# A decoder layer's jobs get times of their own, a third dense buffer, sums on POOL, and multiplications ahead of the first loads

## The reference

```python
# 1: causal linear attention, 16 heads of 64, 128 random features per head
q, k, v = heads(x @ Wq), heads(x @ Wk), heads(x @ Wv)
phi(u) = exp(u @ W_feat - sum(u * u) / 2) / sqrt(128)
y[t] = phi(q[t]) @ sum_{s<=t} outer(phi(k[s]), v[s]) / (phi(q[t]) @ sum_{s<=t} phi(k[s]) + eps)
x = layernorm(x + concat(y) @ Wo)
# 2: differential cross attention to 77 context rows, 16 heads, two softmaxes each
att = softmax(q1 k1) - lam * softmax(q2 k2)
x = layernorm(x + att @ v)
# 3: mixture of 16 experts; a token goes to 4 of them, chosen in 2 of 4 groups, plus a shared expert
weights = 2.5 * normalised sigmoid(x @ gate_w.T) of the chosen four
y = sum_e weights[e] * (silu(x @ Wg[e]) * (x @ Wu[e])) @ Wd[e]
x = layernorm(x + y + shared(x))
```

## Time and profile before

| | |
|---|---|
| median of 3 runs | 997.05 us (994.81 to 1001.26) |
| the profiled execution's own time | 1003.07 us |
| its span | 1001.3 us |
| TensorE busy | 844.2 us, 84% |
| VectorE busy | 667.8 us, 67% |
| ScalarE busy | 497.0 us, 50% |
| POOL busy | 346.1 us, 35% |
| mean granted clock of TensorE | 0.921 |

### The profile page before, as it was taken

One profiled execution on the slowest core, in us unless ns is written; L12 is line 12 of the kernel. 1 busy time (PEld: TensorE's weight loads), 2 busy tenths in 40 slices (PEclk: granted clock), 3 DMA queues, 4 the chain that ended last, 5 costly groups with the idle time before them and its releaser, 6 DMA issues.

```text
span 1001.3 us, 19630 instructions
## 1 busy us (share of the span) xinstructions
PE 844.2 (84%) x6908; PEld 627.8 (63%) x6908; DVE 667.8 (67%) x1714; ACT 497.0 (50%) x1003; POOL 346.1 (35%) x376
## 2 busy tenths in 40 slices
PE   5899978998898899899989989986497876699763
PEld 2578756866676687667768767775275664575331
DVE  4577734457777765777875576877385667664888
ACT  4777744443775443468553437720146753454221
POOL 5211100100583143139415215913314662355121
PEclk9999977999999999999999999997688998799985
DMA  8366565411121133101123221243432322323341
GB/s 297 96 166 172 136 123 139 120 49 50 38 50 52 55 97 87 41 22 31 46 75 107 80 80 32 80 175 129 153 101 91 91 88 71 98 93 113 116 153 72
DMA packets 70158, 96.65 MB, mean 97 GB/s; under 512 B 19632, under 2 KB 50480, under 8 KB 69552
## 3 DMA queue, kind: packets, MB, share of 16 engines
q1 hardware_dynamic: 63408, 78.87, 28.1%
q0 software_dynamic: 5376, 15.47, 4.2%
q10 hardware_dynamic: 1280, 1.05, 0.4%
HBM read 42.33 MB, written 33.10 MB: 75 GB/s over the span
## 4 chain that ended last, share of the span: by engine, by line
PE 49%; DVE 27%; ACT 8%; issue 6%; SPq 5%; DMA 3%; POOL 2%; ACTq 0%; DVEq 0%
PE ps L1517 23%; PE ps L1614 4%; PE ps L1617 4%; PE ps L1595 4%; SPq L692 3%; PE ps L1604 3%; DVE xmax L1378 2%; PE ps L1585 2%; PE ps L1586 2%; PE ps L1587 2%; PE ps L1574 2%; PE ps L1672 1%; DVE low_parts L1323 1%; DVE st L1188 1%; DVE yT L1497 1%
## 5 line engine op out<-in xcount | busy, mean ns | idle before, releaser
L883 POOL TENSOR_TENSOR low_parts<-square,qk 128x512 f16<-128x512 f32 x64 | 76.0, 1187 | 407.4 <-DVE qk L1325 407.3
L1323 DVE SCALAR_TENSOR_TENSOR low_parts<-ps,qk 128x512 f16<-128x512 f32 x64 | 44.1, 689 | 113.8 <-ACT square L974 109.2
L890 POOL TENSOR_TENSOR prob<-prob_full,prob 128x512 f16<-128x512 f32 x84 | 99.3, 1201 | 7.6 <-ACT prob_full L1018 6.2
L912 POOL DMA_INDIRECT rows_out<-attn_mem,dest x64 | 61.8, 966 | 111.2 <-ACT attn_mem L1069 97.5
L1517 PE MATMUL ps<-x_split,w_qkv 128*128 128x512 f16 x384 | 99.3, 397 | 0.9 <-DVE low_parts L1323 0.9
L969 ACT ACTIVATE qk<-ps 128x512 f16<-128x512 f32 x64 | 38.2, 596 | 118.9 <-PE ps L1517 113.4
L1614 PE MATMUL ps<-attn_mem 128*128 128x65 f32 x512 | 93.6, 276 | 2.7 <-issue 2.1
L1614 PEld LDWEIGHTS ps<-attn_mem 128*128 128x128 f32 x512 | 81.0, 197 | 10.8 <-issue 3.1
L1617 PE MATMUL ps<-run,attn_mem 128*128 128x65 f32 x384 | 76.5, 282 | 0.0
L985 ACT ACTIVATE attn_mem<-ps 128x512 f32<-128x512 f32 x64 | 38.5, 602 | 75.6 <-PE ps L1587 74.8
L1595 PE MATMUL ps<-attn_mem 128*128 128x128 f32 x512 | 72.4, 286 | 2.8 <-issue 2.8
(11 more groups left out here) (284 smaller groups left out, 2137.6 us busy)
## 6 DMA issues: line engine op xcount, KB each, us to landing
qk<-low_parts SPq DMA_DIRECT2D x128, 128.0 KB, 2.4
attn_mem<-rows_in SPq DMA_DIRECT2D x64, 144.0 KB, 2.4
late_mem<-ffn_w SPq DMA_DIRECT2D x17, 384.0 KB, 3.8
rows_in<-zero_row SPq DMA_DIRECT2D x32, 144.0 KB, 2.2
up_split<-late_mem SPq DMA_DIRECT2D x16, 256.0 KB, 3.3
x_stage<-xT SPq DMA_DIRECT2D x4, 512.0 KB, 4.4
down_split<-late_mem SPq DMA_DIRECT2D x16, 128.0 KB, 3.6
rows<-x SPq DMA_DIRECT2D x4, 512.0 KB, 4.6
```

The costliest lines, as they stand in the source:

```text
L883: pool.tensor_tensor(low_parts[:, n % 2, 1, :], square[:, n % 2, :], qk[:, n % 2, n // 2 % 2, 0, 1, :], ALU.subtract).then_inc(p_sql.sem, 1)
L890: pool.tensor_tensor(prob[:, n % RING, 1, :], prob_full[:, n % FULL, :], prob[:, n % RING, 0, :], ALU.subtract).then_inc(pr_low.sem, 1)
L912: pool.indirect_dma_start(rows_out[b], bass.IndirectOffsetOnAxis(ap=dest[:, i % YB, j:j + 1], axis=0), yb[:, i % YB, j, :], None).then_inc ...
L1323: dve.scalar_tensor_tensor(low_parts[:, n % 2, 0, :], bank[:, :], 1 / W_SCALE, pair[:, 0, 0, :], ALU.mult, ALU.subtract).then_inc(p_low.se ...
```

## The change

It has four parts.

1. **Jobs timed one by one.** `attention_jobs`, `merged`, `tile_jobs` and `dense_jobs` are gone. Each job gets a time of its own (start of its block or stage plus a number from the tables ATT, CHAIN or END), and the list is sorted by these times. The set of 1,190 jobs is the same.
2. **Three buffers** for the hidden rows of the dense experts in place of two; the weights `wT` move to the memory of `xv` to make room.
3. **Sums on POOL.** Two of the three adds of a `combine` move from VectorE to POOL.
4. **Ahead of the first loads** POOL fills two buffers with ones, and TensorE multiplies them: 12 products on the whole width or on half of the rows, 8 + 16 on 64 and 32 of the array's columns, 6 more on 64 columns. On VectorE a memset and a reciprocal of constants are added at setup step 12. No result uses them.

```diff
-def attention_jobs(t):
...
-    if t + 2 >= 2:
-        add("project", t + 2, H)
-    add("turn keys", t - 1, H)
-    add("q features", t, H)
-    add("state", t - 2, H)
-    add("attend", t - 1, H)
-    if t % 2 == 1:
-        add("turn output", (t - 5) // 2, PAIRS)
-    add("k features", t, H)
-    add("output", t - 3, H)
...
+ATT = dict(project=-1.94, turn_keys=1.1, q_features=0.2, values_0=0.17, values_1=0.17, state=2.57, attend=1.45,
+           turn_output=5.6, k_features=0.36, output=3.73)
+
+CHAIN = dict(out=4.28, out_d=0.239, norm1=5.03, turn=5.55, queries=5.56, scores=6.82, scores_d=0.071, maxima=9.36,
+             probs=9.86, probs_d=0.165, norm2=14.72, cross=15.45, gate=15.84, route0=15.97, up=16.24, route1=17.71,
+             route2=18.29, down=18.08, route3=19.1, prefix=19.61, dispatch=19.62, keep=19.63, ends=20.45)
...
+END = dict(out=-3.81, out_d=1.205, norm1=-0.18, turn=-0.17, queries=-0.16, scores=1.04, scores_d=0.211, maxima=8.72,
+           probs=9.4, probs_d=0.247, norm2=17.99, cross=19.47, gate=20.35, route0=20.52, up=21.03, route1=21.52,
+           route2=21.84, down=22.52, route3=21.85, weights=23.04, dense=23.67, dense_d=2.109, dense_2=1.323,
+           pick=0.65, keep=2.0, sum=4.75, sums=37.0, sums_d=1.0, sums_n=0.77)
...
+    return [job for _, _, job in sorted(jobs)] + end_jobs()
...
-        dense_h = prob_mem[:, 0:1024].rearrange("p (r t) -> p r t", r=2)
-        dense_hT = prob_mem[:, 1024:2048].bitcast(F16).rearrange("p (r a t) -> p r a t", r=2, a=2)
-        wT = prob_mem[0:WROW + NE, 2048:2304].bitcast(F16)
+        dense_h = prob_mem[:, 0:1536].rearrange("p (r t) -> p r t", r=DR)
+        dense_hT = prob_mem[:, 1536:3072].bitcast(F16).rearrange("p (r a t) -> p r a t", r=DR, a=2)
+        wT = xv[0:WROW + NE, :, :, :, :].rearrange("p g c a v -> p (g c a v)")[:, 0:TB]
...
         def _(pool):
+            pool.memset(att[:, :, :, :], 1.0).then_inc(warm.sem, 1)
+            pool.memset(low_parts[:, :, :, :], 1.0).then_inc(warm.sem, 1)
...
+                elif kind == "combine":
+                    i = NT * b + n
+                    four = yg[i % YG]
+                    pool.wait_ge(*yg_loaded[i % YG](i // YG + 1, 0))
+                    pool.tensor_tensor(four[:, 0:2, :], four[:, 0:2, :], four[:, 2:4, :], ALU.add).then_inc(paired.sem, 1)
+                    pool.wait_ge(*paired(i, 1))
+                    pool.tensor_tensor(four[:, 0, :], four[:, 0, :], four[:, 1, :], ALU.add).then_inc(paired.sem, 1)
...
                     act.wait_ge(*dn_gate(0, n + 1))
-                    if n >= 2:
-                        act.wait_ge(*dn_low(0, n - 1))
-                    act.activation(dense_h[:, n % 2, :], bank[:, :], ACT.Tanh, scale=0.5 / W_SCALE).then_inc(dn_tanh.sem, 1)
+                    if n >= DR:
+                        act.wait_ge(*dn_low(0, n - DR + 1))
+                    act.activation(dense_h[:, n % DR, :], bank[:, :], ACT.Tanh, scale=0.5 / W_SCALE).then_inc(dn_tanh.sem, 1)
...
+                if s == 12:
+                    link(dve.memset(prob_full[:, 0:2, :], 1.0))
+                    link(dve.reciprocal(prob_full[:, 2, :], prob_full[:, 1, :]))
...
-                    dve.wait_ge(*yg_loaded[i % YG](i // YG + 1, 0))
+                    dve.wait_ge(*paired(i + 1, 0))
                     four = yg[i % YG]
-                    link(dve.tensor_tensor(four[:, 0:2, :], four[:, 0:2, :], four[:, 2:4, :], ALU.add))
-                    link(dve.tensor_tensor(four[:, 0, :], four[:, 0, :], four[:, 1, :], ALU.add))
                     dve.tensor_tensor(total[:, n, :], four[:, 0, :], total[:, n, :], ALU.add).then_inc(folded.sem, 1)
...
+            pe.wait_ge(*warm(0, 2))
+            for _ in range(2):
+                for h in range(2):
+                    rows = slice(HD * h, HD * h + HD)
+                    pe.matmul(banks[3 + h][:, :], low_parts[rows, 0, 0, 0:P], low_parts[rows, 1, 0, :], start=True, stop=True)
+            for c in range(4):
+                pe.matmul(banks[0][:, P * c:P * c + P], att[:, 0, c, :], att[:, 1, c, :], start=True, stop=True)
...
+            for cols in (64, 32):
+                for c in range(4):
+                    for at in range(0, P, cols):
+                        pe.matmul(banks[2][at:at + cols, P * c:P * c + V1], att[:, 0, c, at:at + cols], att[:, 1, c, 0:V1],
+                                  start=True, stop=True)
```

More of the change, by code:

```diff
@@ L73 @@
 XG, YB, YG = 8, 3, 3
+DR = 3
 WROW = 32
 UP, DOWN = 2, 4
[L79 to L103 removed]
@@ new lines, in chain_jobs @@
+def chain_jobs(put, start, b, at):
+    for n in range(NT):
+        put(start + at["out"] + n * at["out_d"], "project out", b, n)
+    put(start + at["norm1"], "norm1", b, 0)
+    for n in range(2):
+        put(start + at["turn"], "turn stream", b, n)
+    for n in range(KD):
+        put(start + at["queries"], "queries", b, n)
+    for n in range(NT * NG):
+        put(start + at["scores"] + n * at["scores_d"], "scores", b, n)
+    put(start + at["maxima"], "turn maxima", b, 0)
+    for n in range(CHUNKS + LAG):
+        when = start + at["probs"] + n * at["probs_d"]
+        if n < CHUNKS:
+            put(when, "probs", b, n)
+        if n >= LAG:
+            for _, _, m in weighs(b, n - LAG):
+                put(when, "weigh", b, m)
+    put(start + at["norm2"], "norm2", b, 0)
+    for n in range(2):
+        put(start + at["cross"], "turn cross", b, n)
+        put(start + at["up"], "shared up", b, n)
+        put(start + at["down"], "shared down", b, n)
+    put(start + at["gate"], "gate", b, 0)
+    for n in range(4):
+        put(start + at[f"route{n}"], "route", b, n)
+    if b == DENSE:
+        put(start + at["weights"], "weights", b, 0)
+    else:
+        put(start + at["prefix"], "prefix", b, 0)
+        put(start + at["dispatch"], "dispatch", b, 0)
+        put(start + at["keep"], "keep", b, 0)
+        if b == GROUPS[GROUP_OF[b]][-1]:
+            put(start + at["ends"], "ends", GROUP_OF[b], 0)
+            put(start + at["ends"], "table", GROUP_OF[b], 0)
@@ L224, in schedule @@
     first = [(bb, c) for bb in GROUPS[0] for c in range(NT)]
-    ahead = [[] for _ in range(len(first) + 2)]
     for i, (bb, c) in enumerate(first):
-        ahead[i].append(("fetch", bb, c))
-        ahead[i + 2].append(("combine", bb, c))
+        put(END["sums"] + i * END["sums_d"], "fetch", bb, c)
+        put(END["sums"] + (i + 2) * END["sums_d"], "combine", bb, c)
         if c == NT - 1:
-            ahead[i + 2].append(("norm3", bb, 0))
-    rest = [job for part in dense[done:] for job in part]
@@ L232, in schedule @@
-    jobs += merged(rest, [job for part in ahead for job in part])
-    jobs += [("total", DENSE, c) for c in range(NT)] + [("norm3", DENSE, 0)]
-    return jobs
-def dense_jobs(e):
-    jobs = []
-    for kind, k in (("dense gate", e), ("dense up", e), ("dense weigh", e - 1), ("dense keep", e - 1),
-                    ("dense down", e - 2)):
-        if 0 <= k < NE:
-            jobs.append((kind, DENSE, k))
-    return jobs
+            put(END["sums"] + (i + 2) * END["sums_d"] + END["sums_n"], "norm3", bb, 0)
@@ L247, in job_bank @@
+    return [job for _, _, job in sorted(jobs)] + [("total", DENSE, c) for c in range(NT)] + [("norm3", DENSE, 0)]
 def job_bank(kind, b, n):
@@ L562, in decoder_layer @@
         centred = signal("centred")
+        warm = signal("warm")
         t_down = signal("t_down"); t_kept = signal("t_kept")
@@ L1814, in _ @@
                         total = banks[TOTAL_BANKS[c // 2]][:, D * (c % 2):D * (c % 2) + D]
-                        last = three_pass(total, lambda i: dense_hT[:, n % 2, i, P * c:P * c + P],
+                        last = three_pass(total, lambda i: dense_hT[:, n % DR, i, P * c:P * c + P],
                                           lambda j: (d_high, d_low)[j][:, n, :], False, n == NE - 1 and c % 2 == 1)
```

183 lines of the change are left out of this document (68 added, 115 removed).

## The result

The changed kernel takes **936.6 us** (935.20 to 937.98, four runs) against 998.28 us for the kernel before on the same chip: a ratio of 0.938, 95% interval 0.935 to 0.942. Forecast were 971 us and a range of 949 to 990. The profiled execution took 935.2 us, with a span of 933.5 us, so between the two profiles there are 67.8 us to find.

A forecast was written before the change was run, and what follows sets the result against it. It took TensorE to bound the attention blocks, large TensorE holes to mark the expert-tile stretch, VectorE to bound the tail. Terms 12 + 2 + 9 + 3 + 5 - 5 + 0 + 0 = 26 us off 997 gave 971 us, range 949 to 990.

The forecast's parts named there:

- Attention blocks, 5 us: Three attention blocks: reordered jobs close TensorE's waits for keys, a route and the gate; 5 us gain (5 loss to 15 gain).
- My clock term: From 700 to 750 us: shorter holes spare time at half clock, worth some 7 us there alone.
- rival (c): Whole kernel: the holes close, with tail 22, tiles 14, blocks 15 and no block 0 loss; 946 us, chance 0.17.
- Tail, 12 us: Summing of gathered rows: two adds per combine leave VectorE for POOL, less added VectorE waits; 12 us gain (6 to 22).
- Here the third dense buffer counts: Tail: POOL's combine waits for a fetch with a later dense keep behind it; the third buffer was named as help.
- Third buffer, 2 us: Before the first combine: the dense loop may lag one expert more, cutting TensorE's waits for POOL; 2 us gain (0 to 4).
- Last block among the tiles, 9 us (2 to 14): Last block's chain: expert tile jobs put between producers and TensorE consumers shorten waits of gate, probs and weights; 9 us gain.
- End of block 2, 3 us: Where block 2 ends: routing part 2 behind shared down, last output turn ahead of the prefix; 3 us gain (0 to 6).
- Block 0, 5 us loss: Block 0's short steps: early k features wait for moved halves in every second step; 5 us loss (0 to 10).
- Start, 0: Multiplications before the first loads: 2.5 us lost if one after another, 1.5 won if side by side; taken as 0.
- Rival (a): All pairs of steps: features starve waiting for moved halves; slower, 1028 us, middle case 1010 us, chance 0.10.
- (b): Tail and other gains: POOL and VectorE take turns on the shared port, leaving 6 and 3 us; 988 us, chance 0.15.

The follow-up runs named there:

- sums_dve2: The changed kernel with the two adds per combine back on VectorE; ratio to the kernel before 0.9511, first combine to first total 59.8 us.
- pool_only: The kernel before with only the two adds of each combine moved to POOL, two dense buffers and the old order; ratio to the kernel before 1.0139.
- two_rings: The changed kernel with two dense buffers instead of three; ratio to the kernel before 0.9384, first combine to first total 51.7 us.
- late0: The changed kernel with k features behind attend in block 0 only; ratio to the kernel before 0.9337, project out 0 at 186.9 us.
- no_warm2: The changed kernel without the multiplications before the loads and without POOL's two fills for them; ratio to the kernel before 0.9471.
- after_again: The changed kernel itself, run again on another chip as the measure there; ratio to the kernel before 0.9408.

## Why the prediction was right in direction and too small

- **Attention blocks, 5 us: the step that failed.** They gave 32.6 us. The mechanism (a wait closed by distance) is borne out by the waits that are gone; the size was taken from three single waits in the earlier trace rows. Not added up were the idle time of the whole blocks (14.2 + 12.8 + 19.3 us), of which about 15 us went, and the clock of 0.96, 0.97 and 0.95, which is some 40 us at half pace, worth 20 us at most; the busy time fell by 17 us. My clock term stood in rival (c), and there for 700 to 750 us alone. The experiments add that the moves can't be priced one by one: undoing single moves or parts costs 0.8 to 6.0 us in block 1, undoing one of the two halves 14 to 20.
- **Tail, 12 us:** 14.7. POOL's part is 10.0 us (sums_dve2). The price on VectorE was right in kind: six adds lengthened by about 0.95 us, where ten waits of 0.84 were taken, and 2.9 us of waits for POOL's second add. But the term stood as if it needed nothing else; pool_only shows a loss of 14 us without the new places. "Here the third dense buffer counts" named the wrong cover.
- **Third buffer, 2 us:** 1.9 by two_rings, but in another place: before the first combine, where the term stood, two buffers cost nothing (64.2 against 64.3 us).
- **Last block among the tiles, 9 us (2 to 14):** 15.3 from `probs` to `weights`. 12.5 us of it are idle time, near the 12.6 that stood in the sum before the discount. The gate's wait is 1.4 us, that of `weights` 4.7, where under 3 was expected. The same 845 matmuls are busy for 2.8 us less, at a clock of 1.00 instead of 0.91 up to `turn cross`.
- **End of block 2, 3 us:** nothing from project out 3 to scores (34.3 and 34.3), and ahead of it the idle time of block 3 stayed: VectorE's routing mask is no longer waited for (2.3 us before), but the last output turn waits 6.5 instead of 2.9 us. The move of this turn, which the term counted as part of a gain, cost more there.
- **Block 0, 5 us loss:** near the truth, though the two profiles show a gain of 2.9. Project out 0 starts at 182.4 to 188.3 us, mean 184.5, in the eight kernels with k features late in block 0, and at 185.4 to 192.7, mean 188.7, in the twelve with them early. The kernels differ in more than that, and late0 alone did not show it, so the 4 us stay likely and not shown.
- **Start, 0:** 0.7 us in the profile, up to 1.5 by no_warm2. The parts do run beside each other (see the end). Beside the 28 products of 65 columns the term counted ten larger ones; the change has 14 (4 of 512 columns, 4 and 6 of 128). The added memset and reciprocal on VectorE were not tried alone.
- **Rival (a)** did not come: L1584 waits 11.6 us for moved halves, and the same features waited 13.8 us before. **(b)** fell, though six of its twelve turns are there. **(c)**, 946 us at a chance of 0.17, was the right picture and still 9 us short.

## What to carry to other kernels

Before pricing waits one by one, take the idle time and the granted clock of each whole stage: here the clock alone was 24.5 of 67.8 us. Single moves of a schedule may look worthless or small (0.8 and 4.3 us in block 1, where the whole order gave 16.8), because the places depend on each other; try them together. How much of the clock a single hole takes did not come out as a rule here: a hole of 3.0 us was passed at full clock in one run, and one of 1.41 us was not in another. Moving work to an idle engine is worth nothing by itself if that engine's queue also holds a link of the loop that the work belongs to; place the two apart first.

## What the runs showed of the hardware

**Indirect DMAs beside TensorE.** In three of the five batches every kernel that issued a block's 16 indirect DMAs on POOL in one piece, 1.27 us apart, had TensorE stand for 0.3 to 2.4 us between single matmuls that wait for nothing: TensorE's timeline in after_again, then its waits in block 2.

```profile
361.17 0.38 PE L1496 MATMUL ps<-w_o,yT 128*128 128x256 f16 x2 [0.81 <-issue]
362.60 0.27 PE L1496 MATMUL ps<-w_o,yT 128*128 128x256 f16 x1 [1.05 <-issue]
```

```profile
PE ps L1496 <- issue: 7.7, 10, 1.5
```

The three dispatches cost some 40 us in all (39.7 from project out 1 to scores). On the other chips the same instructions ran without a gap. Issued in groups of eight, five and three they cost nothing on either sort. The distance inside a group is the same 1.27 us, so it is not this spacing alone that counts: in all 28 dispatches in one piece on these chips TensorE's first such stand came 7.8 to 11.1 us after the first transfer, beside the seventh to ninth of them, and the last one 20.9 to 22.6 us after it. The groups of eight, whose starts lie within 10.1 us, had none. Why is open.

**Column parts of the array.** In the changed kernel's start 48 matmul records of 65 columns in parts of 64 or 32 took 2.16 us, 0.045 us each (the profile has two records for each fp32 multiplication of the program). The eight over the whole array just ahead took 1.81 us, but they ran at a slow pace: eight of the same size took 1.00 us in block 0 of before, 0.125 each. So the parts are still nearly three times as fast, and the timeline starts them in pairs (64 columns) and fours (32) some 0.007 us apart: they run beside each other. The Trainium skill (TensorEngine Tiling (Array Packing), Key Properties) says that tiles load and multiply in parallel; the trace agrees.

```profile
6.82 1.81 PE L1508 MATMUL ps<-attn_mem 128*128 128x65 f32 x8
8.55 2.16 PE L1512 MATMUL ps<-attn_mem 128*64 128x65 f32 x48
12.04 10.53 PE L1496 MATMUL ps<-w_qkv,x_split 128*128 128x512 f16 x48
```
